# Two-layer graph attention on one core: half a listing before the pair values, pair products a quarter block later, an earlier signal for the first scaling, and another order of the last norms

## The reference, cut to what matters

```python
# layer 0: attention over pairs; only pairs on which adj is set have a score other than 0
att    = (q[sub] * k[obj]).sum(-1) / sqrt(DK)               # 8 heads
scores = zeros.at[:, sub, obj].set(att)                     # -inf where adj == 0, 1e-7 on the diagonal
x      = layernorm(x + softmax(scores).mean(heads) @ x)
# layer 1: 16 heads of leaky_relu(s1[i] + s2[j]), softmax over the ones of adj's row i
hidden = (attn @ (x @ W_seq)) @ W_out + b_out
x      = layernorm(x + elu(hidden))
```

## Time and profile before

| | |
|---|---|
| median of 3 runs | 415.32 us (413.97, 415.32, 416.71) |
| profiled execution, its own time | 415.14 us |
| its span, first to last instruction | 413.4 us |
| PE busy | 362.1 us, 88% of the span |
| DVE busy | 328.6 us, 79% |
| ACT / POOL busy | 205.9 us (50%) / 189.7 us (46%) |
| mean granted PE clock | 0.969 of full speed |

### The profile page before, as it was taken

How to read it: one execution, slowest core, us unless ns; L and a number is a source line. 1 busy time by engine, 2 the same in 40 slices (tenths; PEclk the granted TensorE clock), 3 DMA queues, 4 the chain that set the end, 5 groups by cost and what they waited for, 6 DMA issues and landing times.

```text
span 413.4 us, 5272 instructions
## 1 busy us (share of the span) xinstructions
PE 362.1 (88%) x1638; PEld 198.3 (48%) x1638; DVE 328.6 (79%) x868; ACT 205.9 (50%) x467; POOL 189.7 (46%) x212
## 2 busy tenths in 40 slices
PE   1599999999989898799988982779999999999990
PEld 1155555455344353588777861334444444444450
DVE  0999899876547996777778757689999999999754
ACT  3866756546423121455545431012465667776782
POOL 7777777777510000000000007887877777782000
PEclk9999999999999999899999995889999999999997
DMA  7999253355891330851111126656655767673113
GB/s 253 372 380 376 108 203 103 112 195 141 198 243 59 77 103 1 304 203 59 54 52 57 51 79 170 189 169 181 186 157 157 196 185 217 176 201 106 43 52 133
DMA packets 37063, 65.11 MB, mean 157 GB/s; under 512 B 17953, under 2 KB 19105, under 8 KB 34977
## 3 DMA queue, kind: packets, MB, share of 16 engines
q1 hardware_dynamic: 27936, 42.46, 31.0%
q0 software_dynamic: 9088, 22.20, 19.6%
HBM read 53.50 MB, written 8.52 MB: 150 GB/s over the span
## 4 chain that ended last, share of the span: by engine, by line
PE 46%; POOL 24%; DVE 14%; issue 10%; DMA 2%; ACT 2%; DVEq 0%; SPq 0%; POOLq 0%
POOL pr L504 20%; PE ps L915 16%; PE ps L799 13%; PE ps L832 12%; POOL adjT L593 3%; DVE arenaA L1287 2%; PE ps L788 2%; PE ps L823 2%; DMA adjT<-seqtab,eidx 1%; DMA pr<-in_adj_dram,aidx 1%; PE ps L626 1%; DVE arenaA L1283 1%; DVE arenaC L1719 1%; DVE stats L1725 1%; PE ps L780 1%
## 5 line engine op out<-in xcount | busy, mean ns | idle before, releaser
L593 POOL DMA_INDIRECT adjT<-seqtab,eidx x80 | 81.3, 1016 | 148.9 <-DMA seqtab<-scores 127.0
L626 PE MATMUL ps<-arenaB,adjT 128*128 128x512 f16 x512 | 117.9, 388 | 4.9 <-ACT adjT L975 3.1
L504 POOL DMA_INDIRECT pr<-in_adj_dram,aidx x79 | 81.8, 1035 | 24.0 <-issue 24.0
L915 PE MATMUL ps<-adjT,stage 128*128 128x512 f32 x160 | 79.9, 642 | 13.4 <-DVE adjT L1907 13.4
L626 PEld LDWEIGHTS ps<-arenaB,adjT 128*128 128x128 f16 x512 | 50.0, 100 | 64.9 <-DVE arenaB L1277 3.8
L799 PE MATMUL ps<-stage 128*128 128x272 f32 x256 | 63.0, 400 | 1.5 <-ACT stage L1061 1.5
L1907 DVE TENSOR_TENSOR adjT<-adjT 128x512 f32<-128x512 f32 x80 | 53.8, 734 | 2.2 <-ACT adjT L1187 2.2
L832 PE MATMUL ps<-adjT 128*128 128x512 f32 x120 | 54.0, 592 | 0.0
L799 PEld LDWEIGHTS ps<-stage 128*128 128x128 f32 x256 | 48.4, 194 | 11.3 <-ACT stage L1061 2.1
L915 PEld LDWEIGHTS ps<-adjT,stage 128*128 128x128 f32 x160 | 28.6, 200 | 48.6 <-issue 45.7
L1287 DVE MAX8 arenaA<-arenaA 128x8 f16<-128x256 f16 x120 | 40.7, 411 | 0.5
(11 more groups left out here) (267 smaller groups left out, 492.5 us busy)
## 6 DMA issues: line engine op xcount, KB each, us to landing
stage<-in_adj_dram SPq DMA_DIRECT2D x16, 1024.0 KB
arenaA<-in_x_dram SPq DMA_DIRECT2D x4, 1024.0 KB, 13.3
seqtab<-arenaA SPq DMA_DIRECT2D x16, 256.0 KB, 2.0
out_dram<-arenaC SPq DMA_DIRECT2D x16, 256.0 KB, 3.2
arenaB<-in_x_dram SPq DMA_DIRECT2D x1, 1536.0 KB, 10.7
adjT<-seqtab,eidx POOLq DMA_INDIRECT x80, 3.8
pr<-in_adj_dram,aidx POOLq DMA_INDIRECT x79
arenaC<-in_L_gnn_Wq_dram SPq DMA_DIRECT2D x1, 1024.0 KB, 9.4
```

The costliest lines, as they stand in the source:

```text
L504: g.indirect_dma_start(out=avals[:, t:t + 1], out_offset=None, in_=adj_flat, in_offset=bass.IndirectOffsetOnAxis(ap=aidx[:, t:t + 1], axis ...
L593: g.indirect_dma_start(out=G[:, b % GR, k, :], out_offset=None, in_=seqtab, in_offset=bass.IndirectOffsetOnAxis(ap=eidx[:, b * KE + k:b * ...
L626: ins = t.matmul(bank(4 + b % 2), adjT[:, b, j, :], xsplit[:, w, j, :], start=(j == 0 and w == 0), stop=(j == NB - 1 and w == 1))
L915: t.matmul(bank(2 + b % 2), ehot[:, b % 2, k, :], G[:, b % GR, k, 0:D], start=False, stop=(k == KE - 1), skip_group_check=True)
```

## The change

Four edits. (1) `listing` is cut in two: `list_keys` (key, mask, four of the eight maxima) and `list_top` (the rest). `list_keys(13)` now stands ahead of `count_pairs`, `list_top(13)` behind `fetch_pairs` and ahead of the branch. (2) PE's `pair_offsets` and with it most pair products stand a quarter block (8 matmuls) later, `count_rows` does not, and `pe_sum_flags` comes out of the branch to the place ahead of `pair_scatter`, two quarters into block 15. (3) With few pairs ACT's first scaling and PE's `correct(0)` await `fast_done` in place of `pairs_ready`, which PE awaits later, in place of `wa_made`. (4) At the end ACT makes the roots of rows 12 and 13 together ahead of `elu_part(14)`, puts `norm_of(10)` behind it and runs both halves of the last block one behind the other; DVE does `last_norm(14)` behind the statistics of block 15.

```diff
             for b in range(NB - 1):
                 multiply(b, 0, Q)
-                if b == 11:
-                    pair_offsets()
                 multiply(b, Q, 2 * Q)
...
+                if b == 11:
+                    pair_offsets()
+                multiply(b, 2 * Q, 3 * Q)
                 if b == 11:
                     pair_list()
                 if b == 12:
                     pair_turn()
                 if b == 13:
                     pair_rows()
-                multiply(b, 2 * Q, 3 * Q)
+                if b == 14:
+                    count_rows()
+                multiply(b, 3 * Q, NB)
                 if b == 12:
                     pair_qk()
                 if b == 14:
-                    count_rows()
                     pair_sums()
-                multiply(b, 3 * Q, NB)
...
             multiply(NB - 1, 0, Q)
+            multiply(NB - 1, Q, 2 * Q)
+            pe_sum_flags()
             pair_scatter()
-            multiply(NB - 1, Q, 3 * Q)
+            multiply(NB - 1, 2 * Q, 3 * Q)
...
             def correct(b):
-                if b == 0:
-                    pe.wait_ge(pairs_ready, 1)
                 pe.wait_ge(scaled, b + 1)
...
-                pe.wait_ge(wa_made, 2)
+                pe.wait_ge(pairs_ready, 1)
                 correct(2)
...
             with pe.If(count < FEWER + 1):
-                pe_sum_flags()
+                pe.wait_ge(fast_done, 1)
                 correct(0)
...
             def act_first_norm(last_waits):
-                act.wait_ge(pairs_ready, 1)
+                act.wait_ge(fast_done if last_waits else pairs_ready, 1)
...
                     last_roots(LAST, LAST + 1, LAST // 2)
-                    norm_of(LAST - 2)
-                    elu_part(NB - 2)
                     act.wait_ge(var_made, NB + 2)
                     last_roots(LAST + 1, LAST + 2, LAST // 2 + 1)
-                    elu_half(0)
+                    elu_part(NB - 2)
+                    norm_of(LAST - 2)
+                    for c in range(2):
+                        elu_half(c)
                     act.wait_ge(var_made, NB + 3)
                     last_roots(LAST + 2, LAST + 3, LAST // 2 + 2)
-                    elu_half(1)
                     norm_of(LAST - 1)
...
+            list_keys(NB - 3)
             count_pairs()
             place_pairs()
             fetch_pairs()
+            list_top(NB - 3)

             def last_rows():
-                listing(NB - 3)
                 listing(NB - 2)
...
-                for b in range(LAST + 1, NB - 1):
-                    add_elu(b, late)
-                    last_norm(b - 1, LAST // 2 + b - LAST)
-                add_half(0, late)
+                add_elu(LAST + 1, late)
+                for b in (LAST, LAST + 1):
+                    last_norm(b, LAST // 2 + b - LAST + 1)
+                add_elu(LAST + 2, late)
+                for c in range(2):
+                    add_half(c, late)
+                v.bn_aggr(mv[:, NB - 1, :], stats[:, NB - 2:NB, :]).then_inc(var_made, 1)
                 last_norm(NB - 2, LAST // 2 + NB - 1 - LAST)
-                add_half(1, late)
-                v.bn_aggr(mv[:, NB - 1, :], stats[:, NB - 2:NB, :]).then_inc(var_made, 1)
                 last_norm(NB - 1, LAST // 2 + NB - LAST)
```

More of the change, by code:

```diff
@@ L687, in pair_scatter, with pe_sum_flags @@
                          stop=True).then_inc(scat_made, 1)
+            def pe_sum_flags():
+                pe.wait_ge(bad_made, 1)
+                t.matmul(ps[:, 3, 64:65], ones[:], bad[:, 3:4], start=True, stop=True).then_inc(bad_summed, 1)
             def count_rows():
@@ L863, in pe_dense @@
                         ins.then_inc(L_pe.sem, 1)
-            def pe_sum_flags():
-                pe.wait_ge(bad_made, 1)
-                t.matmul(ps[:, 3, 64:65], ones[:], bad[:, 3:4], start=True, stop=True).then_inc(bad_summed, 1)
             def open_bank(k):
@@ L1260, in _ @@
             links, sp_args = [0], [0]
+            SEG = N // 8
             def link(ins):
@@ L1277, in low, with list_keys @@
                 v.tensor_tensor(xsplit[:, 1, b, :], x_in[:, b, :], xsplit[:, 0, b, :], ALU.subtract).then_inc(low_done, 1)
-            def listing(b, key=key, top=top, junk=junk, offdiag=offdiag):
-                seg = N // 8
+            def list_keys(b, key=key, top=top, offdiag=offdiag):
                 dve.wait_ge(row_cast, b + 1)
@@ L1285, in listing, with list_top @@
                 link(v.tensor_tensor(own, own, offdiag, ALU.mult))
-                for k in range(8):
-                    ins = v.max(top[:, 0, 8 * k:8 * k + 8], key[:, k * seg:(k + 1) * seg])
+                for k in range(4):
+                    v.max(top[:, 0, 8 * k:8 * k + 8], key[:, k * SEG:(k + 1) * SEG])
+            def list_top(b, key=key, top=top, junk=junk):
+                for k in range(4, 8):
+                    ins = v.max(top[:, 0, 8 * k:8 * k + 8], key[:, k * SEG:(k + 1) * SEG])
                 link(ins)
@@ L1294, in listing @@
                                        ALU.mult, ALU.add, deg[:, 1, b:b + 1]).then_inc(row_listed, 1)
+            def listing(b):
+                list_keys(b)
+                list_top(b)
             def score_weights(step):
@@ L1440, in _ @@
             link(v.tensor_scalar(offdiag0, identh[:], -1.0, 1.0, ALU.mult, ALU.add))
-            listing(0, key0, top0, junk0, offdiag0)
+            list_keys(0, key0, top0, offdiag0)
+            list_top(0, key0, top0, junk0)
             for b in range(4, NB):
```

## The result

The changed kernel takes 410.83 us (median of 19 runs, 409.25 to 413.49) against 414.48 us of the kernel before (19 runs, 412.04 to 416.71): a ratio of 0.9931, 95% interval 0.9914 to 0.9949. That is 0.7% faster, inside the forecast range and 0.7 us from the forecast of 411.5. The profiled execution took 410.36 us (span 408.5) where before it was 415.14 (413.4).

The account below looks back on a forecast made before the run. Between 113 and 163 us DVE and PE hand the chain over, neither bounding alone; at the end the stores fill the DMA engines. Gains 1.96 + 1.43 = 3.39 in the middle plus 0.43 at the end, 3.82: 411.5 us, range 409.3 to 414.0.

Parts of the forecast that it names:

- Edit 1, the half: DVE ahead of the pair values: 2.88 us of listing 13 moved into a 3.15 us wait, at no cost.
- The stall: DVE's jump: 6.05 us again from about 122.8, back at 129.0; shorter if DMA traffic made it.
- `attend`: DVE's start of `attend`: 135.17 instead of 137.13, released by PE's `pair_qk`, a gain of 1.96 us.
- Edits 2 and 3: Middle: PE 3.6 us ahead, `pair_qk` not delayed, no wait at `pair_rows`; ACT's scaling 1.43 us earlier by the signal.
- Edit 4: End: last variance 0.89 us earlier, but stores start with `norm_of(11)`, 0.43 us earlier; 0.43 taken for the span.
- The clock: PE's half-speed dip from 168.9 to 172.3: without it 409.7 us, with one more 413.3; chance 0.15, half each way.
- the uncovered half: Rival at the pair values and jump: longer stall or early values exposing the half; 413.0 with 1.5 us; chance 0.16.
- the second fetch: Rival at DVE's jump: two code fetches, 12.1 us, `attend` at 140.4, 416.8 us in all; chance 0.03.
- the end: Rival at the stores: they are not the bound, so the end gives all 0.89 us, 411.0; chance 0.14.

Follow-up runs that it names:

- the listing back: Changed kernel with the whole listing of block 13 behind the jump again; 413.11 us, 0.9957 to the kernel before.
- loads late and turn early: Changed kernel with all `Wx` loads behind block 15's transposing DMA and `pair_turn`, `pair_qk` a quarter earlier; 494.59 us, 0.9964 to the kernel before.

## Why the prediction was right, and where it was not

In sum the forecast gain was 3.82 us and the medians give 3.65. The absolute 411.5 was counted from the median of three runs, 415.32, which with 19 runs is 414.48; that is why it lies 0.7 us above the measured time.

**Edit 1, the half.** Free, as forecast: the wait of 3.15 us is gone, and DVE begins on the values at 112.72 (0.31 earlier than in the kernel before; with the listing back they had landed by 112.74). The forecast idle of 0.3 us is nil in this profile and 0.30 in the second one of the same kernel. POOL at that place, against the earlier trace rows:

```profile
105.33 1.24 POOL L504 DMA_INDIRECT pr<-in_adj_dram,aidx  x1 [0.30 <-issue]
...
109.38 0.95 POOL L504 DMA_INDIRECT pr<-in_adj_dram,aidx  x1 [0.30 <-issue]
110.33 0.91 POOL L507 CAST nearer<-before 128x128 f16<-128x128 f32 x1
```

The last gather keeps its 0.95 us; the copy behind it takes 0.91 beside the early key, 0.30 in the kernel before, and nobody waits for it. By the rule of the Trainium skill that the prediction weighed ("SBUF — State Buffer", "Who interferes with whom") just this copy was to be met, and the trace agrees.

**The stall.** The prediction's 6.05 us run from the end of the branch, and by that count the stall was 5.44 us, not 6.05 again. (The 6.07 in the row of the changed kernel is DVE's whole idle time, which was 7.17 before.) The branch itself came at 121.9 instead of 122.8, so DVE was back at 127.43, 1.6 us ahead of the forecast 129.0. The sentence behind it, that a stall made of DMA traffic would be shorter at a later jump, was the right one. `attend` had 2.62 us to spare at that place instead of 0.9, and so none of this reached the time.

**`attend`.** Forecast at 135.17, released by `pair_qk`. It was released by it at 135.39, since PE waited 1.19 us for the gathered rows instead of 0.72. These 0.22 us are all that the middle missed.

**Edits 2 and 3.** `pair_qk` not delayed, no wait ahead of `pair_rows`, ACT released by DVE's `selfw`: all so, and together exactly 1.43 us. What was wrong is the ledger. The prediction put 1.43 on the signal and none on the quarter; either alone brings 1.2 of it.

**Edit 4.** `norm_of(11)` 0.43 earlier and the last variance 0.89 earlier: measured 0.43 (401.79 - 392.42 against 406.40 - 396.60 is 9.37 and 9.80) and 0.88. For the span I had taken 0.43, with 0.89 as a rival. The first profile says 0.72. But the nine profiles with the new end put the span's end 16.08 to 16.69 us behind the last projection, median 16.43, and the two with the old one 16.80 and 16.74: 0.34 by the medians. The first profile was the luckiest of nine, and a reading from it alone would have favoured the rival. Counted from the end of `norm_of(11)` to the end of the span, the two with the old end show 7.00 and 6.93 us and the nine 6.71 to 7.32, median 7.06; counted from the last norm, 4.40 and 4.32 against 4.56 to 5.17. So the end of the span follows the start of the stream, as the prediction had it, and not the last norm. With the stores in another order the three kernels show 15.69, 15.85 and 16.01 behind the last projection, 0.76 to 1.08 less than with the old end, and 4.16 to 4.49 behind the last norm, as the old end has it: there the stream no longer holds the last store back. That order was not run with the old end, so the split between the two edits isn't shown.

**The clock.** The changed kernel's profile lacks the slow stretch at the start of stage 2; the same kernel profiled again has it:

```profile
163.40:166.80 3.40, 1.70 (x9) 0.95 (x9) 2.05 (x5) 2.12 (x5) 0.00 (x0) 1.00 0.88 276
166.80:170.20 3.40, 3.40 (x18) 2.80 (x17) 2.90 (x8) 0.99 (x2) 0.00 (x0) 1.00 1.01 388
```

```profile
163.40:166.80 3.40, 1.70 (x7) 0.91 (x6) 2.21 (x5) 1.96 (x4) 0.00 (x0) 0.90 0.91 284
166.80:170.20 3.40, 3.40 (x10) 2.58 (x10) 2.90 (x8) 0.99 (x2) 0.00 (x0) 0.60 1.01 383
```

PE was busy 1.70 of 3.40 us in both first stretches, and in one the granted clock fell to half speed (0.50 from 166.50 to 167.50). The first projection took 3.94 us in the changed kernel's profile against 5.41 in the one before; later ones there take 3.83 to 3.93, not the 3.67 that the prediction names, so a dip is worth 1.5 us rather than 1.8. The way from the first correction to the last projection took 232.08 and 232.54 us in the two profiles without it, 232.53 to 234.09 in the eight with it (233.55 in the kernel before, 234.09 in the changed kernel's second profile). The two groups touch, so the dip isn't all of the spread. The 1.01 us in the middle of the first profile are mostly this spread, since the change touches nothing there, and by the traces the change is worth 3.17 + 0.34 = 3.5 us. The medians say 3.65 in the first comparison and 2.14 in the second (412.42 against 414.56).

Of the rivals, the uncovered half and the second fetch didn't happen, and the end gave a part.

## What to carry to other kernels

When work is moved ahead of a jump that must fetch code, read what the DMA engines carry behind it: here the fetch came no sooner than that traffic ended, so bulk loads that nobody needs soon belong behind it. What is put ahead of such a jump comes off the stall: from 7.29 over 5.44 down to 2.75 us in the three kernels that differ only in having none, one or two listings there. Where two edits each cure the same wait, undo them singly before giving either the credit. A term under 1 us is read from positions relative to a common event and from several profiles; here one profile put the end's gain at twice its median.

## What was not expected of the hardware

- A branch cost DVE 2.8 to 7.3 us in kernels that differ only in what lies around it; its code packet needed 0.9 us with the DMA engines idle and up to 5.3 with them full.
- In the kernel before, DMA engines that were nearly idle when the branch ended didn't help: their share was 0.05 and 0.08 in the two half microseconds from 120.0 on, the branch ended at 120.45, the stream began at 121.0, and the packet came at 124.50.
- DVE slows POOL's gathers, too, though only with some operations. Of the 79 gathers of pair values in the kernel before, the 13 that began inside a listing's key (`128x2048`, two inputs) took up to 1.79 us, 1.21 in the median, and the two that began inside a `128x2048` operation of two f32 inputs 2.25 and 2.27; the 42 that began inside maxima, replacements or reductions took 0.94 or 0.95.
- The same gather of pair rows took 6.12 us beside the bulk loads of `Wx` and 4.38 in the kernel with loads late and turn early.
- With a stream that is no longer full, 4.2 to 4.5 us still lie between the last norm and the end of the span; SP waits 3.4 us of these for the last store's completion:

```profile
SPq L54 <- DMA out_dram<-arenaC: 3.4, 1, 3.4
```

- On one chip PE started one matmul every 2.1 to 2.8 us for some 80 us, in the four kernels profiled there. Its cause was not looked into.
